# Feed-forward stage: row-half matmuls, sums taken straight from PSUM, and the mean added and the tiles quantised on other engines

## The reference, cut to what matters

```python
def _L0_ffn_ref(x, weight, bias):
    w_scale = jnp.mean(jnp.abs(weight))
    q_weight = jnp.sign(weight) * (jnp.abs(weight) > 0.5 * w_scale)
    i_scale = jnp.max(jnp.abs(x)) / 127.0          # over the whole tensor
    q_input = jnp.clip(jnp.round(x / i_scale), -128.0, 127.0)
    return jnp.einsum('bsk,ok->bso', q_input, q_weight) * w_scale * i_scale + bias
x = x + _L0_xattn_ref(_layernorm(x), ctx_1024, Wq, Wk, Wv, Wo)
x = x + _L0_ffn_ref(_layernorm(x), weight, bias)
```

## Time and profile before

| | us |
|---|---|
| median of 3 runs (1202.8 to 1204.77) | 1204.3 |
| the profiled execution: its time | 1204.09 |
| its span | 1202.3 |
| feed-forward part: from the first write of a result, 871.77, to the end of the span | 330.5 |
| TensorE busy in the span | 1170.3 (97%) |
| VectorE, ScalarE, GpSimd busy | 1081.4, 1004.3, 755.8 |
| granted TensorE clock, mean | 0.985 |

### The profile page before, as it was taken

How to read it: one execution, slowest core, us unless ns; L and a number is a source line. 1 busy time by engine, 2 the same in 40 slices (tenths; PEclk the granted TensorE clock), 3 DMA queues, 4 the chain that set the end, 5 groups by cost and what they waited for, 6 DMA issues and landing times.

```text
span 1202.3 us, 41935 instructions
## 1 busy us (share of the span) xinstructions
PE 1170.3 (97%) x12471; PEld 946.1 (79%) x12471; DVE 1081.4 (90%) x2410; ACT 1004.3 (84%) x2339; POOL 755.8 (63%) x1536
## 2 busy tenths in 40 slices
PE   7998999999999999999999999999699999999998
PEld 7997999999999999999999999997355555555554
DVE  4654999999999999999999999998688888888887
ACT  4565899999999999999999999998477888888886
POOL 4765999999999999999999999998100000000000
PEclk9999999999999999999999999998699999999999
DMA  9773465656556566565565533330089999999955
GB/s 301 218 198 91 148 185 190 200 173 199 182 192 203 168 198 190 188 200 171 193 201 179 170 105 97 96 93 22 1 313 401 401 400 400 404 401 399 371 209 210
DMA packets 97241, 260.27 MB, mean 216 GB/s; under 512 B 42537, under 2 KB 53993, under 8 KB 76722
## 3 DMA queue, kind: packets, MB, share of 16 engines
q1 hardware_dynamic: 97154, 259.75, 62.6%
q10 hardware_dynamic: 48, 0.07, 0.0%
HBM read 137.11 MB, written 122.64 MB: 216 GB/s over the span
## 4 chain that ended last, share of the span: by engine, by line
POOL 45%; PE 38%; issue 13%; POOLq 1%; DVE 1%; ACT 1%; DMA 0%; SPq 0%; DVEq 0%; ACTq 0%
PE sc_ps L1269 9%; PE pT_ps L1269 9%; POOL qa_sb L546 7%; POOL qb_sb L546 7%; POOL pw_sb L570 6%; POOL rs_sb L555 6%; PE y_ps L1077 5%; PE xT_ps L1260 5%; POOL rs L578 5%; POOL pw_sb L583 4%; POOL os_sb L588 3%; POOL o_sb L590 3%; PE sc_ps L1267 2%; PE pT_ps L1267 2%; POOL mean L596 2%
## 5 line engine op out<-in xcount | busy, mean ns | idle before, releaser
L1222 PEld LDWEIGHTS xT_ps<-wqs,xT_sb 128*128 128x128 f32 x2048 | 239.3, 192 | 49.2 <-ACT xT_sb L702 49.2
L1222 PE MATMUL xT_ps<-wqs,xT_sb 128*128 128x128 f32 x2048 | 263.8, 282 | 3.0 <-ACT xT_sb L702 3.0
L1238 PE MATMUL pT_ps<-v_blk,pT_sb 128*128 128x68 f32 x1536 | 188.9, 273 | 0.0
L1238 PEld LDWEIGHTS pT_ps<-v_blk,pT_sb 128*128 128x128 f32 x1536 | 184.2, 194 | 1.7 <-ACT pT_sb L714 1.1
L939 DVE SCALAR_TENSOR_TENSOR x_sb<-x_sb,mv_sb,y_ps 128x512 f32 (+1 forms) x256 | 177.0, 729 | 4.1 <-PE y_ps L1214 4.1
L1016 DVE TENSOR_TENSOR x_sb<-x_sb 128x512 f32 (+1 forms) x256 | 164.6, 683 | 1.2 <-ACT x_sb L760 1.2
L665 ACT ACTIVATE sq_sb<-x_sb 128x512 bf16 (+1 forms) x256 | 163.4, 638 | 1.2 <-DVE x_sb L939 0.8
L946 DVE TENSOR_REDUCE amax<-x_sb (+1 forms) x128 | 154.2, 1205 | 0.0
L760 ACT ACTIVATE x_sb<-pT_ps,mean,cols 128x512 f32<-128x512 f32 x128 | 99.5, 778 | 63.5 <-PE pT_ps L1269 63.1
L702 ACT ACTIVATE xT_sb<-xT_ps 128x512 f32<-128x512 f32 x256 | 139.2, 597 | 2.9 <-PE xT_ps L1144 2.8
L724 ACT ACTIVATE e_sb<-e_sb,rs_sb 128x308 f32<-128x308 f32 x256 | 127.3, 544 | 11.0 <-DVE e_sb L914 7.4
(11 more groups left out here) (135 smaller groups left out, 2508.7 us busy)
## 6 DMA issues: line engine op xcount, KB each, us to landing
out_y<-x_sb SPq DMA_DIRECT2D x112, 1024.0 KB, 6.5
x_sb<-in_x SPq DMA_DIRECT2D x128, 512.0 KB, 3.8
x_sb<-out_y SPq DMA_DIRECT2D x48, 1024.0 KB, 9.1
x_sb<-in_ctx SPq DMA_DIRECT2D x38, 256.0 KB, 4.3
k_blk<-k_scr SPq DMA_DIRECT2D x256, 9.6 KB, 1.7
v_scr<-x_sb SPq DMA_DIRECT2D x38, 68.0 KB, 2.8
k_scr<-x_sb SPq DMA_DIRECT2D x38, 64.0 KB, 3.2
v_blk<-v_scr SPq DMA_DIRECT2D x128, 10.2 KB
```

The lines of the kernel that those rows point to most:

```text
L1222: last = pe.matmul(bank[0][:, t * HD:(t + 1) * HD], xT_sb[:, t, c, :], wqs[:, c, :], start=c == 0, stop=c == EC - 1)
L1238: last = pe.matmul(bank[6][:, at0:at0 + 2 * VC], pT_sb[:, t, c * P:(c + 1) * P], v_blk[:, slot, c, c:c + 2, :].rearrange("p h d -> p (h d) ...
```

## The change

TensorE's work in the feed-forward part is cut into row halves. A pair of tiles is transposed by 16 transposes of 64 rows into two banks, one for each half. Each matmul over 128 rows becomes two over 64: the first pass multiplies rows 0 to 63 of tile `2m` beside rows 64 to 127 of tile `2m+1`, the second pass the other halves. The transposes of the next batch stand between the passes, and the second pass waits for the end of the first (`ffn_half`). The bias needs one matmul of 64 rows a tile, in the first pass only; for that its operands are copied to rows 64 and on, once. `q_T` and `ffn` have banks of their own for each `m`, and `q16T_sb` and `u_sb` hold two batches.

ScalarE no longer reads PSUM. It quantises all four tiles, two batches ahead, and adds the mean to tiles 0,1 from SBUF to SBUF. GpSimd adds it to tiles 2,3 in one instruction of 1024 elements. VectorE no longer quantises; its add takes the sum from PSUM, scales it and adds `u_sb` in one instruction, into `x1_sb`. The attention part and the SyncE list stay as they are.

```diff
-        u_sb = x_sb[:, 1, :, :]
+        u_sb = x_sb[:, 1:3, :, :]
...
+            def add_mean(g, k, back):
...
+                at_least(pool, sum_done_t, 4 * (j - 2) + TPB)
+                at = (j - SLOTS if back else j + B - KEPT) * TPB + 2
+                pool.tensor_tensor(u_sb[:, k % 2, 2:4, :],
+                                   x1_sb[:, bass.ds(x1_turn(g, k) + 2 * E, 2 * E)].rearrange("p (t e) -> p t e", t=2),
+                                   mean1[:, bass.ds(at, 2)].unsqueeze(2).broadcast_to([P, 2, E]),
+                                   ALU.add).then_inc(mean_23, 1)
...
-            def scale_out(g, k, back):
...
-                    act.activation(u_sb[:, t, :], bank[4 + t][:, :], ACT.Identity,
-                                   bias=stat_of(mean1, j, t, back), scale=cols[:, 6:7]).then_inc(scaled_t, 1)
...
+                at_least(act, qT2_done, 2 * j - 1 + m)
+                for t in range(2 * m, 2 * m + 2):
+                    act.activation(qm_sb[:, m, t % 2, :], x1_sb[:, bass.ds(x1_turn(g, k) + t * E, E)], ACT.Copy,
...
+                for t in range(2):
+
+                    at_least(act, sum_done_t, 4 * (j - 2) + t + 1)
+                    act.activation(u_sb[:, k % 2, t, :], x1_sb[:, bass.ds(x1_turn(g, k) + t * E, E)], ACT.Identity,
+                                   bias=stat_of(mean1, j, t, back)).then_inc(mean_01, 1)
...
+                dve.tensor_scalar(q16T_sb[:, 4 * par + 2 * m:4 * par + 2 * m + 2, :, :].rearrange("p t c (n r) -> p (t c) n r", n=2),
+                                  ps[:, :, 0:E // 2].bitcast(F16).rearrange("p n (b r) -> p b n r", r=HALF),
                                   -HALF_OFFSET, None, ALU.add).then_inc(qT2_copied, 1)
...
-                dve.tensor_tensor(x1_tile, x1_tile, u_sb[:, t, :], ALU.add).then_inc(sum_done_t, 1)
...
+                dve.scalar_tensor_tensor(out=x1_sb[:, bass.ds(x1_turn(g, k) + t * E, E)], in0=bank[4 + t][:, :],
+                                         scalar=cols[:, 6:7], in1=u_sb[:, k % 2, t, :], op0=ALU.mult,
+                                         op1=ALU.add).then_inc(sum_done_t, 1)
...
-                        last = pe.transpose(bank[m][:, at0:at0 + P // 2].bitcast(F16), q16[:, ::2], ident16[:, :])
+                        for n in range(2):
+                            lo, hi, at0 = n * HALF, (n + 1) * HALF, (t * EC + c) * HALF // 2
+                            q16 = qm_sb[lo:hi, m, t, c * P:(c + 1) * P].bitcast(F16)
+                            last = pe.transpose(bank[2 * m + n][:, at0:at0 + HALF // 2].bitcast(F16), q16[:, ::2],
+                                                ident16[lo:hi, lo:hi])
...
+            def ffn(j, par, m, second):
+
+                if second:
+                    pe.wait_ge(ffn_half, 4 * j + 2 * m + 2)
+                else:
+                    at_least(pe, sum_done_t, 4 * j + 2 * m - 2)
+                    pe.wait_ge(qT2_copied, 2 * j + m + 1)
+                    for n in range(2):
+                        rows = slice(n * HALF, (n + 1) * HALF)
+                        pe.matmul(bank[4 + 2 * m + n][:, :], bones[rows, :], brow[rows, :], start=True, stop=False)
                 for c in range(EC):
...
+                    for n in range(2):
+                        rows, t = slice(n * HALF, (n + 1) * HALF), 2 * m + (n ^ second)
+                        last = pe.matmul(bank[4 + t][:, :], q16T_sb[rows, 4 * par + t, c, :], wT[rows, c, :], start=False,
+                                         stop=second == 1 and c == EC - 1)
...
                 for m in range(2):
...
+                    ffn(j, par, m, 0)
                     if more:
                         q_T(j + 1, m)
...
+                    ffn(j, par, m, 1)
```

More of the change, by code:

```diff
@@ L599, in _ @@
             steps(pool, step)
+            def add_mean(g, k, back):
+                j = g * XS + k
+                if back:
+                    pool.wait_ge(x1_in[k], (g - RING) * 16 + 16)
+                at_least(pool, sum_done_t, 4 * (j - 2) + TPB)
[4 more added lines that the diff above has]
+                                   ALU.add).then_inc(mean_23, 1)
+            pool.wait_ge(scale_ready, 1)
+            pool.wait_ge(mean_ready, NP_)
+            for j in range(SLOTS):
+                add_mean(j // XS, j % XS, False)
+            with pool.Fori(RING, B // XS) as g:
+                for k in range(XS):
+                    add_mean(g, k, True)
         @block.scalar
@@ L739, in _, with quantise @@
             act.wait_ge(mean_ready, NP_)
-            def quantise(g, k, back):
+            def quantise(g, k, m, back):
                 j = g * XS + k
@@ new lines, in _, with turn @@
+            for m in range(2):
+                quantise(0, 0, m, False)
+            for m in range(2):
+                quantise(0, 1, m, False)
+            add_mean(0, 0, False)
+            def turn(g, k, back):
+                j = g * XS + k
+                left = B - j if isinstance(j, int) else B
+                if left > 2:
+                    quantise(g + (k + 2) // XS, (k + 2) % XS, 0, back)
+                if left > 1:
+                    add_mean(g + (k + 1) // XS, (k + 1) % XS, not isinstance(j, int) or j + 1 >= SLOTS)
+                if left > 2:
+                    quantise(g + (k + 2) // XS, (k + 2) % XS, 1, back)
@@ L1032, in turn @@
+            def turn(g, k):
                 j = g * XS + k
@@ L1035, in turn @@
                     if left > 1:
[L1036 to L1038 removed]
+                        unoffset(j + 1, m, (k + 1) % 2)
                     for t in range(2):
                         add(g, k, 2 * m + t)
[L1042 to L1045 removed]
+            unoffset(0, 0, 0)
+            unoffset(0, 1, 0)
             for j in range(SLOTS):
[L1047 removed]
+                turn(j // XS, j % XS)
             with dve.Fori(RING, B // XS - 1) as g:
                 for k in range(XS):
[L1050 removed]
+                    turn(g, k)
             for j in range(B - XS, B):
[L1052 removed]
+                turn(j // XS, j % XS)
         @block.tensor
@@ new lines, in q_T @@
+                last.then_inc(qT2_done, 1)
+            def ffn(j, par, m, second):
[7 more added lines that the diff above has]
+                        pe.matmul(bank[4 + 2 * m + n][:, :], bones[rows, :], brow[rows, :], start=True, stop=False)
+                for c in range(EC):
+                    for n in range(2):
+                        rows, t = slice(n * HALF, (n + 1) * HALF), 2 * m + (n ^ second)
+                        last = pe.matmul(bank[4 + t][:, :], q16T_sb[rows, 4 * par + t, c, :], wT[rows, c, :], start=False,
+                                         stop=second == 1 and c == EC - 1)
+                        if c == EC - 1 and not second:
+                            last.then_inc(ffn_half, 1)
+                if second:
+                    last.then_inc(ffn_done, 1)
@@ L1275, in _, with batch @@
             pe.wait_ge(bias_ready, 1)
-            def batch(j, more=True):
+            def batch(j, par, more=True):
                 for m in range(2):
-                    for t in range(2):
-                        ffn(j, 2 * m + t)
+                    ffn(j, par, m, 0)
                     if more:
                         q_T(j + 1, m)
-            batch(0)
-            with pe.Fori(1, B - 1) as j:
-                batch(j)
-            batch(B - 1, False)
+                    ffn(j, par, m, 1)
+            batch(0, 0)
+            with pe.Fori(0, (B - 2) // 2) as h:
+                for n in range(2):
+                    batch(h * 2 + (n + 1), (n + 1) % 2)
+            batch(B - 1, 1, False)
 def kernel(**inputs):
```

75 lines of the change are left out of this document (24 added, 51 removed).

## The result

The changed kernel takes 1185.5 us (median of 4 runs, 1181.85 to 1187.1) against 1203.55 of the kernel before beside it (4 runs, 1202.33 to 1204.77): ratio 0.9846, interval 0.9819 to 0.9873, so 18 us faster. Repeated later it took 1184.72, ratio 0.9854 [0.9838, 0.987]. The profiled execution took 1181.85 with a span of 1180.0. The time lies in the forecast range, 5.5 above the likeliest 1180, but the reasons are not those of the likeliest case, as the profile shows; that the number came so near is in part luck.

What follows compares the result with a forecast made beforehand. TensorE was taken as the bound at 5.21 us a batch, transfers only just hidden. First write 870.2, then 63 batches of 4.83, less 0.94, plus 0.4, gave 1174.0; plus 4.4 and 1.8, 1180.2. Range 1170 to 1200.

Steps and rivals of the forecast that it cites:

- the likeliest case: Feed-forward part: TensorE sets the pace at 4.83 us a batch, giving 1180 us; chance 0.68.
- A pair at 0.216: TensorE's feed-forward matmuls: two 64-row halves of 512 columns stream at once and cost one matmul, 0.216 us.
- The step of 0.35 in the attention part: Attention part's 512-column matmul pairs: 0.35 us from pair to pair, taken as the upper end for a feed-forward pair.
- the rival of pairs that overlap only in part: TensorE's 512-column pairs: at 0.24 us each the time is 1207, at 0.35 it is 1332; chance 0.09.
- The transposes at 0.47: TensorE, each half batch: sixteen 64-row transposes take 0.47 us, near the attention part's measured 0.52 in fp32.
- Rival 2: Feed-forward part: transposes overlap (0.22 us), TensorE falls to 4.33 a batch, the transfers end last at 1170; chance 0.08.
- The floor of the transfers at 1170: Feed-forward reads and writes: at 5.21 us a pair they end at 1170, deciding when a batch takes under 4.67.
- The first write at 870.2: Start of the feed-forward part: the first result write comes at 870.2, 1.6 us earlier than before.
- rival 5: Feed-forward loop: each GpSimd add holds VectorE for its 2.5 us, 6.8 a batch and 1304 us; chance 0.03.
- GpSimd's add at 2.5: GpSimd's mean add of 1024 elements, each batch: 2.28 ns an element and 2.5 us, costed at nothing.
- VectorE bound by a slower unoffset: VectorE reading two banks in pieces of 64: unoffset grows to about 1.2 us, time 1211 or 1200; chance 0.07.
- The waits between the passes: TensorE's second pass waits for the first: 0.16 us to cover, hidden by 0.47 of transposes except in the last batch.

Runs made afterwards that it cites:

- e3: The changed kernel with TensorE's matmuls and transposes over all 128 rows again, the new division of labour kept: 1204.9 us, 1.0018 of the kernel before.
- e1_pool_late: The changed kernel with GpSimd's first mean add waiting until the bias is ready: 1183.1 us, 0.984 of the kernel before.
- e4: The changed kernel with TensorE's row halves kept but the old division of labour between ScalarE and VectorE: 1298.0 us, 1.0789 of the kernel before.
- e9_lag4: The changed kernel with reads four batches behind writes instead of two, eight semaphores per direction, loops written out: 1173.2 us, 0.9756 of the kernel before.
- the best version: The changed kernel with reads four batches behind, late GpSimd start, earlier bias-row copy, first two results written by halves: 1170.0 us, 0.9723 of the kernel before.
- e5_transfers_alone: The changed kernel without any feed-forward compute, only its 64 writes and 48 reads of 1 MB: 1142.1 us.

## Why the prediction was right, and where it was not

- **What bounded the kernel before: right.** TensorE at 5.21 a batch, with the new division alone worth nothing (e3).
- **A pair at 0.216: right**, exactly. The step of 0.35 in the attention part was no measure for fp16; the rival of pairs that overlap only in part is out.
- **The transposes at 0.47: wrong.** They take 0.25, in pairs 29 ns apart. The step that failed is "32 ns apart in fp32 looks more like a price for each instruction than for its columns": 29 ns is about half of the earlier trace rows's 56 for 128 columns, as if two streamed at a time at the rate of their columns, and the two transposes of a pair, on different halves of the array, start 4 to 5 ns apart. The rows had this already: an fp32 matmul of 128 columns cost 0.128 us, so 64 columns an estimated 0.064, and eight pairs of them 0.51, where 0.52 was measured. The term was 0.22 too large twice a batch: 4.83 predicted, 4.41 measured.
- **So the likeliest case, TensorE at 4.83, was not what happened.** Rival 2 was, in kind: below 4.67 the transfers end last. Its chance of 0.08 was too low, since it hung on the transposes; and its time, 1170, was 15 under the measured one.
- **The floor of the transfers at 1170: right in kind, wrong in its rate and in holding that rate constant.** Its rate of 402 GB/s, read as a limit since the share was near 1, was only what TensorE asked for; 427 is possible. The rows below,'s view again, give what is lost against 427: 134.89 x 20 / 427 = 6.3 us until 1010, at 407 GB/s; 120 x 53 / 427 = 14.9 in the slow stretch, at 374 (its row stands above); 1.1 until 1171, and 9 x 356 / 427 = 7.5 in the last 9 us, at 71. With the transfers' own 117.4 MB / 427 = 275 that makes the 305 us from first write to end. The prediction had 298 from first write to end of the span (1170, less the 1.8 around it, less 870.2). Two errors of opposite sign nearly met, the rate too low, and a slow stretch and a lagging DMA engine that I had not thought of, and that is luck, as is the nearness of 1180, the time of a case that did not happen.

```profile
875.11:1010.00 134.89, 134.89 (x2080) 69.97 (x2078) 122.53 (x184) 115.84 (x185) 58.70 (x31) 1.00 0.98 407
...
1130.00:1171.00 41.00, 22.53 (x304) 10.58 (x300) 20.64 (x30) 15.34 (x25) 7.58 (x4) 0.84 1.01 416
1171.00:1180.00 9.00, 0.00 (x0) 0.00 (x0) 0.00 (x0) 0.00 (x0) 0.00 (x0) 0.50 0.17 71
```

- **The first write at 870.2: 875.1.** Half of this is no error of a term: this execution's attention part ended 2.4 later (L1006 at 857.23; the line that was L973 started at 854.85), and in the repetition the first write came at 871.28. GpSimd's hold on VectorE is another 2.8, and the other terms came out 0.3 shorter.
- **GpSimd blocks VectorE (rival 5): in the loop no, at the start yes.** The add is 0.746 where I had 0.729. The prediction looked at the new adds, which have one input in PSUM, and forgot the preparation of the bias, where the two operations that were held have two tensor inputs in SBUF: 1.71 and 1.40 us against 0.15 in `e1_pool_late`. That these inputs make the difference fits the 0.20 and 0.14 of the two operations with one, but no run varied the inputs alone.
- **GpSimd's add at 2.5: 1.89**, 1.85 ns an element and not 2.28. It costs nothing either way.
- **VectorE bound by a slower unoffset: no.** 0.680 against 0.691 before; two banks in pieces of 64 cost nothing here.
- **The waits between the passes: as predicted, hidden**, although the cover is 0.25 and not 0.47. That the transposes there need ScalarE two batches ahead, I passed over in half a sentence; without the new division of labour the kernel is 113 us slower (e4).

## What to carry to other kernels

When a change lifts the pace of the engine that bounds, recompute the transfers as the next bound at a rate from a stretch in which they queue; a DMA share near 1 beside landings of 7 to 9 us was no limit. When a transfer's landing releases the next one, keep enough queued beyond it, and look at when the last of its sixteen counts comes, not only the middle one (11.4 us apart in `e9_lag4`): one number (`LAG` from 2 to 4) was worth 9 of the 33 us that the best version gains. When work moves between two passes of an engine, check how far ahead its inputs are made, and by an engine that waits for which pass.

## What the runs showed of the hardware

- Transposes of 64 rows and 64 columns in fp16, alternating between the array's halves, came in pairs 29 ns apart, the two of a pair 4 to 5 ns apart (the sixteen at 1002.40 of the changed kernel, 0.25 us); pairs of 64-row matmuls of 512 columns took 0.216 us each, as one over 128 rows did before.
- Transfers of 1 MB in both directions, with nothing else at work, moved 427 GB/s from 900 to 1130 and 420 over all 279.9 us, with a median of 309 ns for a packet of 8 KB (`e5_transfers_alone`).
- With the queue full and the engines at work, the last of a landing's sixteen counts came 11.4 us after the middle one between 1110 and 1130 (`e9_lag4`), and the last 13 us of the run moved 30 GB/s; with no engine at work it came 1.5 us after (`e5_transfers_alone`). That this is one of sixteen DMA engines falling behind is a reading of these numbers.
- A VectorE operation of nine elements with two tensor inputs in SBUF took 1.71 us, and another 1.40, beside GpSimd adds of 1.89 (each 0.15 without them, `e1_pool_late`); the VectorE add with one input in PSUM took 0.746 from 900 to 1100, where GpSimd was busy for 85.2 of 200 us.
